# A cosine threshold moved from two matmuls to products on ScalarE and GpSimd and a subtraction on VectorE

## The reference

```
m = h @ map_w.T + map_b
sem = m.reshape(b, s, h, dk).transpose(0, 2, 1, 3)
norm = jnp.maximum(jnp.linalg.norm(sem, axis=-1, keepdims=True), COS_EPS)
n = sem / norm
cos = jnp.einsum('bhsd,bhtd->bhst', n, n)
cos_adj = (cos > THRESHOLD).astype(embs.dtype)
...
p_attn = jax.nn.softmax(scores, axis=-1) * keep
adj = cos_adj * p_attn
Ax = jnp.einsum('hbst,hbtd->hbsd', adj_h, sem_h)
```

## Time and profile before

| | |
|---|---|
| median of 3 runs | 2514.99 us (2514.61 to 2515.3) |
| profiled execution, its own time | 2513.98 us |
| span of the profile | 2512.1 us |
| busy: TensorE, VectorE, ScalarE, GpSimd | 98%, 81%, 69%, 82% |
| DMA engines, mean busy share | 60.3% on SP's queue |
| granted TensorE clock | 0.997 of full speed |

### The profile page before, as it was taken

One profiled execution on the slowest core, in us unless ns is written; L12 is line 12 of the kernel. 1 busy time (PEld: TensorE's weight loads), 2 busy tenths in 40 slices (PEclk: granted clock), 3 DMA queues, 4 the chain that ended last, 5 costly groups with the idle time before them and its releaser, 6 DMA issues.

```text
span 2512.1 us, 77339 instructions
## 1 busy us (share of the span) xinstructions
PE 2472.5 (98%) x29880; PEld 1976.2 (79%) x29880; DVE 2023.7 (81%) x3426; ACT 1740.7 (69%) x4528; POOL 2052.0 (82%) x2330
## 2 busy tenths in 40 slices
PE   8899999999999999999999999999999999999997
PEld 6777877878878878778778778778788787787785
DVE  6888888788788787888788887887887878888876
ACT  5676676676676776766766766766767767667665
POOL 4788888888888888888888888888888888888875
PEclk9999999999999999999999999999999999999999
DMA  5566565666666656665656666656566566556643
GB/s 154 96 123 117 119 122 117 124 120 120 127 116 122 128 115 126 125 118 118 131 116 121 120 121 122 123 117 127 116 122 128 114 123 130 115 120 128 117 91 73
DMA packets 840557, 300.56 MB, mean 120 GB/s; under 512 B 782464, under 2 KB 790144, under 8 KB 840192
## 3 DMA queue, kind: packets, MB, share of 16 engines
q1 hardware_dynamic: 840192, 295.62, 60.3%
HBM read 75.80 MB, written 33.55 MB: 44 GB/s over the span
## 4 chain that ended last, share of the span: by engine, by line
PE 93%; DVE 2%; ACT 1%; POOL 1%; issue 1%; DMA 1%; SPq 0%; POOLq 0%; ACTq 0%; DVEq 0%
PE unit_ps L2064 26%; PE unit_ps L1886 26%; PE unit_ps L1900 25%; PE s_ps L1910 4%; PE s_ps L1969 4%; PE c_ps L1910 3%; PE unit_ps L2036 2%; PE unit_ps L1910 2%; PE c_ps L1942 1%; PE unit_ps L1980 1%; ACT e_ec L939 0%; DMA e_ec<-in_L_gnn_q_w_dram 0%; DVE e_ec L1280 0%; DMA ec_t<-e_ec 0%; POOL e_ec L734 0%
## 5 line engine op out<-in xcount | busy, mean ns | idle before, releaser
L939 ACT ACTIVATE e_ec<-e_ec,neg_mx 128x128 f32<-128x128 f32 x1008 | 390.0, 388 | 4.1
L2064 PE MATMUL unit_ps<-m_hl,w_q_hi 128*128 128x256 f16 x2048 | 356.7, 273 | 0.0
L2064 PE MATMUL unit_ps<-m_hl,w_k_hi 128*128 128x256 f16 x2048 | 355.7, 273 | 0.6 <-DVE qk_sb L1316 0.6
L1035 ACT ACTIVATE qk_hl<-qk_sb 128x512 f16<-128x512 f32 x256 | 153.3, 622 | 286.5 <-DVE qk_sb L1316 286.5
L1886 PE MATMUL unit_ps<-h_t,w_m_hi 128*128 128x256 f16 x2048 | 339.6, 273 | 2.8 <-DVE qk_sb L1316 1.5
L1900 PE MATMUL unit_ps<-w_v_hi,h_t 128*128 128x512 f16 x1024 | 325.4, 379 | 0.0
L996 ACT ACTIVATE h_sb<-x,shift,rstd 128x512 f32<-128x512 f32 x128 | 104.1, 814 | 267.2 <-POOL shift L809 267.2
L1886 PE MATMUL unit_ps<-h_t,w_m_lo 128*128 128x256 f16 x1024 | 279.3, 273 | 0.0
L734 POOL TENSOR_TENSOR e_ec<-e_ec 128x1024 f16<-128x1024 f32 x126 | 269.0, 2135 | 2.1 <-ACT e_ec L969 2.1
L1280 DVE SCALAR_TENSOR_TENSOR e_ec<-c_ps,e_ec 128x1024 f32<-128x1024 f32 x126 | 154.3, 1225 | 112.4 <-ACT e_ec L939 112.4
L2064 PE MATMUL unit_ps<-m_hl,w_q_lo 128*128 128x256 f16 x1024 | 237.5, 273 | 0.0
(11 more groups left out here) (280 smaller groups left out, 7540.8 us busy)
## 6 DMA issues: line engine op xcount, KB each, us to landing
xa<-in_x_dram SPq DMA_DIRECT2D x128, 256.0 KB, 3.4
x<-in_x_dram SPq DMA_DIRECT2D x128, 256.0 KB, 3.0
out_dram<-x SPq DMA_DIRECT2D x128, 256.0 KB, 2.4
h_t<-h_hl SPq DMA_TRANSPOSE x254, 3.4
ec_t<-e_ec SPq DMA_TRANSPOSE x252, 3.2
adj_in<-in_adj_dram SPq DMA_DIRECT2D x128, 16.0 KB, 2.1
norm_t<-norm_parts SPq DMA_TRANSPOSE x128, 2.3
p_t<-p_hl SPq DMA_TRANSPOSE x126, 3.3
```

What stands on the lines that cost most here:

```text
L939: ins = nc.scalar.activation(e[:, h, :], e[:, h, :], ACT.Exp, bias=neg[:, h:h + 1], scale=SCALE, accum_out=sums[:, h:h + 1])
L1035: nc.scalar.activation(dst[:, 0, c, :], src[:, c, :], ACT.Copy).then_inc(done, 1)
L2064: ins = nc.tensor.matmul(ps[:, c % 2 * 2 * P:(c % 2 + 1) * 2 * P], w[a][:, i, c * P:(c + 1) * P], parts[:, b, i, :], start=n == 0, stop=n ...
```

## The change

The norms are no longer split, transposed and multiplied by TensorE. After the power, SP stores the 128x16 norms into a DRAM tensor `norm_d`, head by head (graph, head, node), so that each of the 2048 numbers goes to a place of its own, waits until they have landed, and loads each graph's 1024 numbers into all 128 partitions of `norm_n` (`keep_norms`, `spread_norms`, in the place of `turn_norms`). A partition then holds the norms of all nodes t of all heads. `threshold` multiplies them by the partition's own norm of each head: for the even graph on ScalarE (eight activations, one per head, ahead of `scores_exp` in the even slot), for the odd graph on GpSimd (one product, behind `block_mask` in the odd slot). `above` on VectorE subtracts the products from `c_ps` in place, and `gate` waits for it. The norms stand in the order graph, half, head instead of half, graph, head (the pattern of `out` in `norms`). Four small constants tiles and their preparation go.

```
+        norm_d = nc.dram_tensor("norm_d", (2, H, P), F32).ap()
+        norm_n = sb("norm_n", [P, 2, H, P])
...
+            def keep_norms(s):
+                if s.has(1):
+                    sp.wait_ge(norm_done, s.at(lambda t: (t + 1) // 2 + 1))
...
+                    for g in range(2):
+                        wait(sp, norm_in[g], s.at(lambda t: 16 * ((t + 1) // 2)))
...
+                    sp.dma_start(norm_d.rearrange("g h n -> n (g h)"), norm[:, :],
+                                 allow_slow_non_contiguous=True).then_inc(norm_kept, 16)
+
+            def spread_norms(s):
+                if s.has(1):
+                    wait(sp, lowered, s.at(lambda t: t + 1))
...
+                    sp.wait_ge(norm_kept, s.at(lambda t: 16 * ((t + 1) // 2 + 1)))
+                    for g in range(2):
+                        sp.dma_start(norm_n[:, g].rearrange("p h n -> p (h n)"),
+                                     norm_d[g].rearrange("(a h) n -> a (h n)", a=1).broadcast_to([P, H * P])).then_inc(norm_in[g], 16)
...
                     turn_e(s, 0, e_hi)
-                    turn_norms(s)
+                    keep_norms(s)
+                    spread_norms(s)
                     turn_e(s, 1, e_lo)
```

```
+                    wait(pool, norm_kept, s.at(lambda t: 16 * ((t + 1) // 2)))
+                    for g in range(2):
+                        wait(pool, threshold_done[g], s.at(lambda t: (t + 1) // 2))
                     nc.gpsimd.tensor_tensor(norm[:, :], sq_sum[:, :], plus_half[:, :], ALU.pow).then_inc(norm_done, 1)
-                    wait(pool, norm_in, s.at(lambda t: 32 * ((t + 1) // 2)))
...
-                    nc.gpsimd.tensor_copy(parts[:, :, 1:4, :], rows.unsqueeze(2).broadcast_to([P, 2, 3, 2 * C])).then_inc(norm_split, 1)
...
+            def threshold(s):
+                if s.has(0):
+                    pool.wait_ge(norm_in[1], s.at(lambda t: 16 * (t // 2 + 1)))
+                    pool.wait_ge(norm_done, s.at(lambda t: t // 2 + 1))
+                    nc.gpsimd.tensor_tensor(norm_n[:, 1], norm_n[:, 1],
+                                            norm[:, H:2 * H].unsqueeze(2).broadcast_to([P, H, P]),
+                                            ALU.mult).then_inc(threshold_done[1], 1)
```

ScalarE, VectorE and TensorE:

```
+            def threshold(s):
+                if s.has(0):
+                    act.wait_ge(norm_in[0], s.at(lambda t: 16 * (t // 2 + 1)))
+                    act.wait_ge(norm_done, s.at(lambda t: t // 2 + 1))
+                    for h in range(H):
+                        ins = nc.scalar.activation(norm_n[:, 0, h, :], norm_n[:, 0, h, :], ACT.Copy, scale=norm[:, h:h + 1])
+                    ins.then_inc(threshold_done[0], 1)
...
+            def above(s):
+                if s.has(0):
+                    dve.wait_ge(c_full, s.at(lambda t: t + 1))
+                    dve.wait_ge(threshold_done[s.n % 2], s.at(lambda t: t // 2 + 1))
+                    cosine = c_ps[:, :, :].rearrange("p a (b n) -> p (a b) n", b=4)
+                    nc.vector.tensor_tensor(cosine, cosine, norm_n[:, s.n % 2], ALU.subtract).then_inc(lowered, 1)
...
                     dve.wait_ge(e_done, s.at(lambda t: t + 1))
-                    dve.wait_ge(c_full, s.at(lambda t: t + 1))
+                    dve.wait_ge(lowered, s.at(lambda t: t + 1))
...
-                    pe.wait_ge(threshold_done, s.at(lambda t: t // 2 + 1))
-                    for a in range(2):
-                        r = slice(a * DK, (a + 1) * DK)
-                        ins = nc.tensor.matmul(c_ps[:, a, :], norm_t[r, 0, :], norm_r[r, s.n % 2].rearrange("p c n -> p (c n)"),
-                                               start=False, stop=True)
-                    ins.then_inc(c_full, 1)
+                              columns(s.n % 2)).then_inc(c_full, 1)
```

More of the change, by code:

```diff
@@ L395, in build @@
         norm_done = sem("norm_done")
-        norm_split = sem("norm_split")
-        norm_in = sem("norm_in")
-        threshold_done = sem("threshold_done")
+        norm_kept = sem("norm_kept")
+        norm_in = [sem(f"norm_in{i}") for i in range(2)]
+        threshold_done = [sem(f"threshold_done{i}") for i in range(2)]
+        lowered = sem("lowered")
         masked = sem("masked")
@@ L828, in slot @@
                     block_mask(s)
+                    threshold(s)
                     x_lower(s)
@@ L889, in _ @@
             block_mask(z)
+            threshold(z)
             o1_lower(z, 5)
@@ L899, in _ @@
             h1_lower(a)
+            threshold(b)
             v_lower(a)
@@ L1204, in _ @@
             h1_upper(z)
+            threshold(a)
             scores_exp(a)
@@ L1407, in square_rest @@
                                                    op0=ALU.mult, op1=ALU.add).then_inc(sq_lo, 1)
-            def threshold_rows(s):
-                if s.has(1):
-                    dve.wait_ge(norm_in, s.at(lambda t: 32 * ((t + 1) // 2 + 1)))
-                    wait(dve, c_full, s.at(lambda t: t + 1))
-                    nc.vector.tensor_tensor(norm_r[:, :, :, :].rearrange("p g c n -> p (g c) n"),
-                                            norm_t[:, 1, :].unsqueeze(1).broadcast_to([P, 2 * C, P]),
-                                            norm_mask[:, :].unsqueeze(2).broadcast_to([P, 2 * C, P]),
-                                            ALU.mult).then_inc(threshold_done, 1)
             def attended(s):
@@ L1493, in first_slot @@
                 x_stats(s)
+                above(s)
                 gate(s)
@@ L1523, in slot @@
                     k_lower(s, 1)
-                    threshold_rows(s)
                     lqk_lower(s, "lk", lk_hl, LK, 1)
@@ L1749, in _ @@
             dve.wait_ge(ones_in, ONES)
-            threshold_rows(before_0)
-            dve.wait_ge(ones_in, ONES)
             over_slots(dve, B, slot)
@@ L1756, in _ @@
             o1_rows(z, 5)
+            above(z)
             q_features(z, 1)
@@ L1766, in _ @@
             x1_stats(z)
-            threshold_rows(z)
             lqk_lower(z, "lq", lq_hl, LQ, 0)
             scores_mask(a)
+            above(a)
             scores_mask(b)
@@ L1774, in _ @@
             x1_stats(a)
+            above(b)
             gate(b)
@@ L1902, in rows, with row_pairs @@
                 return ins
-            def row_pairs(outs, mv, st, cols, last=True):
+            def row_pairs(outs, mv, st, cols):
                 for c in range(len(outs[0])):
@@ L1910, in row_pairs @@
                             ins = nc.tensor.matmul(outs[half][c], st[r, a, c, cols], mv[r, b, c, cols],
-                                                   start=n == 0 and (last or c == 0), stop=last and n == 2)
+                                                   start=n == 0, stop=n == 2)
                 return ins
@@ L1937, in cosines @@
                     row_pairs([[c_ps[:, a, c * P:(c + 1) * P] for c in range(C)] for a in range(2)], parts, parts,
-                              columns(s.n % 2), last=False)
-                    pe.wait_ge(threshold_done, s.at(lambda t: t // 2 + 1))
-                    for a in range(2):
-                        r = slice(a * DK, (a + 1) * DK)
-                        ins = nc.tensor.matmul(c_ps[:, a, :], norm_t[r, 0, :], norm_r[r, s.n % 2].rearrange("p c n -> p (c n)"),
-                                               start=False, stop=True)
-                    ins.then_inc(c_full, 1)
+                              columns(s.n % 2)).then_inc(c_full, 1)
             def l1_scores(s):
@@ L1977, in norms @@
                     for g in range(2):
-                        out = ps[:, 0:2 * H].rearrange("p (a g c) -> p g a c", a=2, g=2)[:, g]
+                        out = ps[:, 0:2 * H].rearrange("p (g a c) -> p g a c", a=2, g=2)[:, g]
                         for n, (c, part) in enumerate((c, part) for c in range(C) for part in range(2)):
```

35 lines of the change are left out of this document (5 added, 30 removed).

## The result

| | before | after |
|---|---|---|
| median of 4 runs each, side by side | 2515.14 us (2514.61 to 2516.93) | 3019.97 us (3014.06 to 3027.31) |
| profiled execution: its time, its span | 2513.98, 2512.1 us | 3023.86, 3022.0 us |
| granted TensorE clock | 0.997 | 0.942 |
| mean distance of one pair's power from the next, 9th to 62nd | 38.14 us | 46.10 us |

The ratio is 1.200, 95% interval 1.199 to 1.202: 505 us slower, where 87 were forecast. 7.96 us a pair over some 62 pairs is 494 of them.

A forecast was written before the change was run, and what follows sets the result against it. TensorE, busy 98%, was taken to bound the kernel at 38.14 us a pair. A loop of 29.9 + 9.6 = 39.5 us adds 1.36 over 62 pairs, 84 us, plus 2 to 3 at the end: 2602 us, range 2505 to 2800.

The forecast's parts named there:

- the term of the store: Writing 2048 norms to DRAM, issue to landing: 5.1 us taken, 3.0 of it for elements; bounds 2.1 and 12.5.
- R, the cost no row shows: Prediction's section sizing the norms' round trip through DRAM: store 5.1, load 4.2, semaphores 0.3, together 9.6 us.
- rival 3: Store near its upper bound: loop 46.9 us, about 3063 us; chance 0.13, including all round trips over 12 us.
- R: Time from norms on GpSimd to the first half of the spread in SBUF (store, wait, load): 9.6 us, ends 5.4 and 18.8.
- If the store lands after 8 us or more, the mechanism stands and R is mis-sized: Sign to look for in the profile after; the forecast itself expected a store landing in about 5 us.
- The 14 ns: Time per single element, from reads in a 1 us DMA window: 16 x 0.55 / 640; 128 elements per engine need 1.8 us.
- The loop: From GpSimd's new product through power, round trip, ScalarE's products, exponentials and p_lower back: 29.9 + 9.6 = 39.5 us a pair.
- The second loop: Circle without DMAs, through GpSimd's layer norm, ScalarE's h1 steps and both products: 38.5 us, longer than today's 38.14.
- rival 2: TensorE stays the bound, both products run in holes, and 34 us are gained: 2480 us; chance 0.12.
- The first step: Odd slot: later second q eviction stops TensorE before the k matmuls some 0.9 us a pair; about 1.9 in the sum.
- The weighted sums, costed at nothing: Even slot: e transpose lands 5 to 6 us later, but its user on TensorE starts 9.7 us after today's issue.
- The other terms: Rest of the round trip: load of 512 KB 4.2 us, two semaphores 0.3, SP taken as free for the store.

The follow-up runs named there:

- e4: Changed kernel plus three rounds of ten small transfers behind its last wait, each waited for; 2048 single elements to DRAM landed after 10.1 us.
- e10: Changed kernel with norms stored as 1024 pieces of 8 bytes and read with steps of 8 bytes; 2664.07 us, ratio to before 1.059.
- e3: Changed kernel with ScalarE's products reading a constant tile, not waiting for the loads; even graphs' values wrong; 2802.19 us, ratio to before 1.114.
- e6: Changed kernel with a contiguous store (256 pieces of 32 bytes), loads and users unchanged, mask not the reference's; 2507.04 us, ratio to before 0.996.
- e2: Changed kernel with SP issuing the norm loads behind the transpose of e's low half and the result's store; 3056.34 us, ratio to before 1.215.
- e5: Changed kernel plus ten small transfers per round, varying piece size and spacing; 128 elements of 4 bytes took 7.7 us side by side, 1.4 spaced 64 bytes.
- e9: Changed kernel plus eleven small DRAM stores per round, varying spacing; 128 elements 4, 8 and 16 bytes apart took 7.5, 3.4 and 1.4 us.
- e13: Changed kernel plus seven small DRAM stores per round, varying element count; 16, 32 and 128 elements side by side took 1.3, 3.1 and 7.1 us.

## Why the prediction was wrong

**The step that failed** is the term of the store in "R, the cost no row shows": "I take 3.0, the store 5.1". It measured 10.5. The 3.0 were sized from 14 ns an element by reads the earlier trace rows, and for the sending they were more than enough: in e4 the engines send their 128 elements each in 1.3 us, 10 ns an element, and in the kernel the last packet leaves 2.7 us after the issue. What had no row was the time from the last packet to the report, 7.8 us. The text said that "ours are writes to DRAM" and took a value near the lower bound all the same; between ends of 2.1 and 12.5 with no row for a write, the range should have reached the upper one. That one gave rival 3 at R = 17.0 and 3063 us, which is near what came, with a chance of 0.13 for it and all above R = 12. That it came near is luck: it was scaled up by the number of elements, and e4 has 7.0 us for 128 of them and 10.1 for 2048. The sign named beforehand, "If the store lands after 8 us or more, the mechanism stands and R is mis-sized", is the one that showed.

The 14 ns rest on a wrong reading of the earlier trace rows too. By the packet records that window holds 74 packets of 4 bytes, 64 of 256 and 47 of 512, not 640 short ones; the two column loads had sent nearly all of their elements before it, 1018 packets of 4 bytes between 6.75 and 8.25 us.

The Trainium skill (DMA: Bandwidth & Descriptors, Rules for kernel authors) had warned against a strided last dimension. These runs bear it out. The price that the Trainium skill has in the section Bandwidth of that page, 10.5 ns a packet, is that of sending. The 10 ns of e4 agree with it. In the section Latency and other measured facts the Trainium skill puts a transfer's fixed cost at about 2 us, mostly the receipt from the memory written. The 1.5 us of e4's pieces of 32 bytes and more agree with that, the 7.0 us of 128 neighbouring elements do not.

**The loop** was right. Without R its parts took 29.58 us in the mean of 53 pairs of the changed kernel and 29.66 in e10, where 29.9 were taken: GpSimd to the end of the power 7.37 (7.1 taken), ScalarE's products up to the exponentials 2.35 (2.56), GpSimd's product 1.90 (2.3). They stay as they are while the mean R goes from 16.51 to 10.76 and the pair from 46.10 to 40.43. e3 shows that the changed kernel is bound by it.

**The second loop** was too long by 0.7 us at the least, and with it fell the claim that the change "cannot be hidden even if its DMAs cost nothing": in e6 the pair is 37.84, under the 38.14 of before. GpSimd's product and ScalarE's products make 0.6 of it. So rival 2 had the sign right for a quick store.

**The first step** overstated TensorE's stop: 69.4 us in the changed kernel and 12 in e6 in front of the k matmuls, 1.1 and 0.2 a pair, where 1.9 was forecast.

**The weighted sums, costed at nothing.** They waited 4.0 us a pair and the clock fell in that wait; that this lies "inside a loop that is then longer anyway" was right: e2 took that wait away and gained nothing.

**The other terms** of R: the loads took 4.65 (4.2 taken), and 0.97 passed between the power and the store, where 0.3 stood for both semaphores and SP was taken to be free. The subtraction took 1.23 (1.3).

## What to carry to other kernels

A store that something waits for is priced to its report, not to the end of its packets: where no row of the trace shows such a store, give its upper bound real weight. Write to DRAM in longer pieces than single numbers and let the reader step: steps of 8 bytes cost VectorE and GpSimd nothing and ScalarE 15 ns of 387, steps of 32 bytes cost all three a quarter to two thirds more. A wait on a queue that issues everything is filled with the transfers that are due in the meantime, not moved to where it holds up others.

## What was not expected of the hardware

- Writes of neighbouring partitions to neighbouring addresses in DRAM: 128 of 4 bytes side by side land after 6.8 to 8.5 us (e4, e5, e9, e13), 8 bytes apart after 2.8 to 3.4, 16 bytes apart after 1.4 (e9); 16 of them side by side after 1.3. In e4 and in the kernel the DMA engines are idle for the 7.8 us before the report.
- The same 2048 elements from tile to tile land after 2.9 us.
- In a stop of 4.8 us TensorE's granted clock fell to 0.50, and it still stood there 3 us after the stop in the pair shown. The stop itself cost nothing: e2 took it away and was no faster, since another loop was longer.
